# Layer 1's experts computed only for the two chosen per token, through a list sorted by expert

## The reference

```python
logits = jnp.einsum('th,eh->te', x, router_w)            # 8 experts
topk_logits, topk_idx = jax.lax.top_k(logits, K)         # K = 2
probs = jax.nn.softmax(topk_logits, axis=-1)
combine = combine.at[jnp.arange(T)[:, None], topk_idx].add(probs)
hmid = jax.nn.gelu(jnp.einsum('th,efh->etf', x, w1) + b1[:, None, :])   # 128 -> 256
y = jnp.einsum('etf,ehf->eth', hmid, w2) + b2[:, None, :]               # 256 -> 128
out = jnp.einsum('eth,te->th', y, combine)
```

## Time and profile before

| | |
|---|---|
| median of 3 runs | 1991.66 us (1989.51 to 1996.56) |
| profiled execution: span | 1994.7 us |
| token stage of layer 1, first matmul to the attention's first | 1142.1 to 1444.5 us |
| attention of layer 1 | 1444.5 us to the end |
| busy: PE, DVE, ACT, POOL | 86%, 67%, 60%, 57% of the span |
| HBM traffic | 67 GB/s over the span |

### The profile page before, as it was taken

One profiled execution on the slowest core, in us unless ns is written; L12 is line 12 of the kernel. 1 busy time (PEld: TensorE's weight loads), 2 busy tenths in 40 slices (PEclk: granted clock), 3 DMA queues, 4 the chain that ended last, 5 costly groups with the idle time before them and its releaser, 6 DMA issues. The chain is left out here.

```text
span 1994.7 us, 78600 instructions
## 1 busy us (share of the span) xinstructions
PE 1724.8 (86%) x34080; PEld 1310.1 (66%) x34080; DVE 1335.0 (67%) x1975; ACT 1194.0 (60%) x1438; POOL 1128.4 (57%) x1489
## 2 busy tenths in 40 slices
PE   6887789999999989999988689999967878788886
PEld 4666678777787777778766566667635555555554
DVE  5552777777777758877776244544477888777882
ACT  2333477777787768777876534444425656566565
POOL 4755589987899769987995522221012333334333
PEclk9988799999998999999998789999958999999898
DMA  3476032222322222222112122133112112121100
GB/s 111 124 212 173 24 96 76 76 71 76 88 69 80 62 76 83 86 70 70 48 59 69 58 68 82 58 91 97 54 26 50 31 49 48 37 59 31 26 24 17
DMA packets 166301, 139.91 MB, mean 70 GB/s; under 512 B 91715, under 2 KB 157014, under 8 KB 160454
## 3 DMA queue, kind: packets, MB, share of 16 engines
q1 hardware_dynamic: 150966, 100.40, 17.2%
q10 hardware_dynamic: 9616, 21.89, 4.5%
q0 software_dynamic: 5376, 12.59, 2.2%
HBM read 90.91 MB, written 43.12 MB: 67 GB/s over the span
## 5 line engine op out<-in xcount | busy, mean ns | idle before, releaser
L1364 ACT ACTIVATE a_EX<-bank 128x1024 f32<-128x1024 f32 x624 | 615.4, 1026 | 288.9 <-PE bank L1236 235.0
L1490 DVE TENSOR_TENSOR a_PM<-bank,a_PM 128x1024 f32<-128x1024 f32 x336 | 401.7, 1221 | 129.2 <-PE bank L1236 118.0
L1316 POOL TENSOR_TENSOR a_SN<-a_SN,a_MB 128x1024 f32<-128x1024 f32 x176 | 421.0, 2429 | 48.0 <-DMA a_MB<-m_dram 47.2
L1513 DVE TENSOR_REDUCE a_M<-bank 128x2 f32<-128x1024 f32 (+3 forms) x304 | 339.0, 1163 | 82.0 <-PE bank L1249 53.3
L1453 PE MATMUL bank<-a_EX,VV 128*32 128x128 f32 x9984 | 359.7, 288 | 6.5 <-issue 4.9
L1236 PE MATMUL bank<-QS,KS 51*128 51x128 bf16 (+1 forms) x4992 | 234.9, 228 | 93.9 <-DMA QS<-a_MP 29.9
L1453 PEld LDWEIGHTS bank<-a_EX,VV 128*32 128x32 f32 x9984 | 269.8, 114 | 51.0 <-issue 22.7
L1236 PEld LDWEIGHTS bank<-QS,KS 51*128 51x128 bf16 (+1 forms) x4992 | 156.7, 99 | 185.8 <-issue 52.0
L1360 ACT ACTIVATE a_SN<-bank 128x1024 f32<-128x1024 f32 x176 | 176.7, 1024 | 57.6 <-PE bank L1215 56.3
L1368 ACT ACTIVATE a_SN<-a_SN 128x1024 f32<-128x1024 f32 x176 | 184.9, 1060 | 34.7 <-POOL a_SN L1316 34.7
L1215 PE MATMUL bank<-QP,rel_t 112*128 112x32 bf16 x5632 | 197.9, 177 | 3.0 <-issue 2.7
(11 more groups left out here) (163 smaller groups left out, 2410.2 us busy)
## 6 DMA issues: line engine op xcount, KB each, us to landing
a_MB<-m_dram SPq DMA_DIRECT2D x32, 1024.0 KB, 5.0
QS<-q_dram SPq DMA_DIRECT2D x192, 96.0 KB, 2.9
KS<-k_dram ACTq DMA_DIRECT2D x16, 768.0 KB
q_dram<-t_PARTS SPq DMA_DIRECT2D x32, 192.0 KB, 2.8
k_dram<-t_PARTS SPq DMA_DIRECT2D x16, 384.0 KB, 2.9
QS<-a_MP SPq DMA_DIRECT2D x384, 2.0 KB
KR<-kr_dram ACTq DMA_DIRECT2D x8, 576.0 KB
q_dram<-t_PARTS SPq DMA_DIRECT2D x32, 128.0 KB, 2.6
```

What stands on the lines that cost most here:

```text
L1316: pool.tensor_tensor(near_view(sn), near_view(sn), as_near(MB[:, :, :], it.part), ALU.add)\
L1364: act.activation(as_banks(EX[:, it.need % ER[layer]], part), by_head, ACT.Exp, scale=SCALE).then_inc(act_done, 1)
L1490: dve.tensor_tensor(pm, mb.rearrange("p hh (k i) -> p hh k i", k=4), pm, ALU.max).then_inc(max_used, 1)
L1513: dve.tensor_reduce(target.rearrange("p (hh k) -> p hh k", hh=2)[:, :, p0:p0 + g], mb[:, :, 0:g * width].rearrange("p hh (k j) -> p hh k j ...
```

## The change

Layer 1's token stage is replaced (`routed_stage`); the other three stages keep their order. Layer 1's tokens are now normalised in two chunks of 2048 tokens (16 tiles) instead of groups of 512; the first chunk is prepared in the seam, the second one by DVE inside the stage. For each chunk, all logits come first; DVE picks the two experts for 16 tiles at once, and PE counts, with matmuls against tables of zeros and ones (`places`), where in a list sorted by expert each token's two copies go. Each expert's part of the list is filled up to whole tiles of 128 rows, so that the list has 39 tiles ("steps") per chunk, 78 in all, whatever the data. POOL scatters each tile of tokens twice into the list in DRAM, by 64 indirect transfers of 128 rows; the list was filled with zeros by 26 transfers of SP during layer 0's attention. Then the experts are computed step by step. SP loads the list four steps at a time (a "quad"), PE turns them, and the number of the expert of each step is read by PE, ACT and DVE from SBUF into registers, once per quad on each engine. DVE copies the expert's w1 (128x256) to a ring of four buffers for PE's weights; b1, w2 and b2 are addressed by register. DVE adds b2, SP stores the result. All of q, k and v, with their split, runs between the routing and the experts, with the differences of the split now on DVE. In the attention, POOL gathers a unit's two result rows per token with two indirect transfers and one plain one, four units ahead, mixes them (`mix`, three operations) and applies the silu with ACT's tanh (`gate`, two operations); DVE's multiplication in `final` waits for it. g_dram and the sum over 8 experts are gone for layer 1.

The diff, cut and moved to the left; first what is removed, then `routed_stage` in the order POOL, SP, ACT, PE, DVE, then the attention:

```diff
-if kind == "expert" and layer == 1:
-    if k + 1 < E:
-        hidden(f, p, k + 1)
-    elif not (f == GROUPS - 1):
...
-for t in range(GT):
-    y = bank[:, YB + k % 2, t * P:(t + 1) * P]
-    for h in range(2):
-        last = pe.matmul(y, HM[:, k % 2, h, t * P:(t + 1) * P], w2[:, k, h, :],
-                         start=h == 0, stop=h == 1)
...
-dve.wait_ge(y_psum, f * E + k + 1)
-for t in range(GT):
-    last = dve.scalar_tensor_tensor(ACC[:, p, t, :], bank[:, YB + k % 2, t * P:(t + 1) * P],
-                                    C[:, p, t, k:k + 1], ACC[:, p, t, :], ALU.mult, ALU.add)
...
+def experts_of(engine, c, q):
+    size = quad_size(q)
+    _, values = nc.values_load_multi_w_load_instructions(step_e[0:1, c, 4 * q:4 * q + size], engines=[engine],
+                                                         min_val=0, max_val=E - 1)
+    return values
...
+for c in range(CHUNKS):
+    pool.wait_ge(slots_ready, c + 1)
+    for t in range(CT):
+        for k in range(2):
+            at = SLOT[:, k, c * CT + t:c * CT + t + 1]
+            pool.indirect_dma_start(out=xs_dram[c], out_offset=bass.IndirectOffsetOnAxis(ap=at, axis=0),
+                                    in_=X1[c][:, t, :], in_offset=None).then_inc(scattered[c], 16)
...
+def load_slots(q):
+    c, i = divmod(q, QUADS)
+    sp.wait_ge(scattered[c], 16 * 2 * CT)
+    if q >= 3:
+        sp.wait_ge(xs_psum, q - 2)
+    size = quad_size(q)
+    sp.dma_start(XS[:, q % 3, 0:size, :], xs_dram[c].rearrange("(s p) d -> p s d", p=P)[:, 4 * i:4 * i + size, :])\
+      .then_inc(xs_in[q % 3], 16)
...
+for to, src in loads:
+    sp.dma_start(to, src).then_inc(route_in, 16)
+load_chunk(sp, 1)
+for to, src in expert_loads:
+    sp.dma_start(to, src).then_inc(expert_in, 16)
+sp.wait_ge(v_ones, 1)
+for f in range(GROUPS):
+    store_v(f)
+    store_qk(f)
+    if f == 5:
+        for q in range(3):
+            load_slots(q)
+for u in range(QR):
+    load_q(1, sp, u)
+for q in range(CHUNKS * QUADS):
+    store_y(q)
+    if q + 3 < CHUNKS * QUADS:
+        load_slots(q + 3)
...
+def first_part(f):
+    if f >= 2:
+        act.wait_ge(qk_stored[f % 2], QKS * (f // 2))
+    act.wait_ge(qk_taken, 2 * f + 2)
...
+for f in range(1, GROUPS):
+    values(f)
+    first_part(f)
+    second_part(f - 1)
+second_part(GROUPS - 1)
...
+if s >= 3:
+    act.wait_ge(y_psum, s - 2)
+for h in range(2):
+    last = act.activation(HM[:, s % 3, h, :], bank[:, HB + s % 3, h * P:(h + 1) * P], ACT.Gelu,
+                          bias=b1[:, bass.ds(e, 1), h:h + 1].rearrange("p a f -> p (a f)"))
+last.then_inc(hid_ready, 1)
...
+def hidden(q, k, s):
+    pe.wait_ge(xs_ready, q + 1)
+    pe.wait_ge(w_ready, s + 1)
+    if s >= 3:
+        pe.wait_ge(hid_ready, s - 2)
...
+for h in range(2):
+    last = pe.matmul(bank[:, HB + s % 3, h * P:(h + 1) * P], W[:, s % 4, h * P:(h + 1) * P], XST[:, q % 2, k, :],
+                     start=True, stop=True)
...
+def result(q, k, s, e):
+    pe.wait_ge(hid_ready, s + 1)
+    if s >= 3:
+        pe.wait_ge(y_ready, s - 2)
+    for h in range(2):
+        last = pe.matmul(bank[:, YB + s % 3, 0:P], HM[:, s % 3, h, :],
+                         w2[:, bass.ds(e, 1), h, :].rearrange("p a f -> p (a f)"), start=h == 0, stop=h == 1)
+    last.then_inc(y_psum, 1)
...
+for f in range(CG):
+    if f + 1 < CG:
+        turn(f + 1)
+    logits(f)
+project(0)
+pe.wait_ge(route_in, 16 * len(loads))
+places(0)
...
+for f in range(CG, GROUPS):
+    if f + 1 < GROUPS:
+        turn(f + 1)
+    logits(f)
+places(1)
+for f in range(1, GROUPS):
+    project(f)
...
+for i in range(QUADS):
+    q = c * QUADS + i
+    if q + 1 < CHUNKS * QUADS:
+        turn_slots(q + 1)
+    for k, e in enumerate(experts_of(mybir.EngineType.PE, c, i)):
+        s = step_index(c, 4 * i + k)
+        hidden(q, k, s)
+        if len(behind) == 2:
+            result(*behind.pop(0))
+        behind.append((q, k, s, e))
...
+def second_rest(f):
+    dve.wait_ge(p1_ready, f + 1)
+    dve.tensor_tensor(FR[:, f % 2, :, :], FQ[:, f % 2, :, :], PARTS[:, f % 2, 0, :, :], ALU.subtract).then_inc(r_ready, 1)
...
+def weights(s, e):
+    if s >= 4:
+        dve.wait_ge(hid_psum, s - 3)
+    dve.tensor_copy(W[:, s % 4, :], w1[:, bass.ds(e, 1), :].rearrange("p a f -> p (a f)")).then_inc(w_ready, 1)
...
+def add_bias(q, k, s, e):
...
+dve.tensor_tensor(Y[:, q % 3, k, :], bank[:, YB + s % 3, 0:P], b2[:, bass.ds(e, 1), :].rearrange("p a f -> p (a f)"),
+                  ALU.add).then_inc(y_ready, 1)
...
+dve.wait_ge(route_in, 16 * len(loads))
+route(0)
+chunk_statistics(dve, 1)
+dve.drain()
+rsqrt(dve, rstd1[:, :], var1[:, :], newton1[:, :], fused=True)
+chunk_normalise(dve, 1)
+dve.drain()
+route(1)
+for f in range(GROUPS):
+    take(f)
+    if f:
+        third_part(f - 1)
+    second_rest(f)
+third_part(GROUPS - 1)
...
+slots(q)
+for k, e in enumerate(experts_of(mybir.EngineType.DVE, c, i)):
+    s = step_index(c, 4 * i + k)
+    weights(s, e)
+    if len(behind) == 3:
+        add_bias(*behind.pop(0))
+    behind.append((q, k, s, e))
...
+if 2 <= u < 2 + CHUNKS * STEPS // 3:
+    sp.wait_ge(zeros_ready, 1)
+    c, s0 = divmod(3 * (u - 2), STEPS)
+    sp.dma_start(xs_dram[c].rearrange("(s p) d -> p s d", p=P)[:, s0:s0 + 3, :],
+                 bv[:, None, :].broadcast_to([P, 3, D])).then_inc(zeroed, 16)
...
+r, tile = u % XGR, row_of(u)
+for i in range(3):
+    pool.wait_ge(y_out[i], 16 * len(range(i, (tile // CT + 1) * QUADS, 3)))
+if u >= XGR:
+    pool.wait_ge(final_done, u - XGR + 1)
...
+for k in range(2):
+    pool.indirect_dma_start(out=XG[:, r, 1 + k, :], out_offset=None, in_=y_dram[tile // CT],
+                            in_offset=bass.IndirectOffsetOnAxis(ap=SLOT[:, k, tile:tile + 1], axis=0))\
+        .then_inc(xg_in[r], 16)
+pool.dma_start(XG[:, r, 0, :], x_v[tile]).then_inc(xg_in[r], 16)
...
+def mix(u):
+    r, tile = u % XGR, row_of(u)
+    pool.wait_ge(xg_in[r], 48 * (u // XGR + 1))
+    pool.tensor_scalar(XG[:, r, 1, :], XG[:, r, 1, :], PW[:, 0, tile:tile + 1], None, ALU.mult)
+    pool.tensor_scalar(XG[:, r, 2, :], XG[:, r, 2, :], PW[:, 1, tile:tile + 1], None, ALU.mult)
+    pool.drain()
+    pool.tensor_tensor(XG[:, r, 1, :], XG[:, r, 1, :], XG[:, r, 2, :], ALU.add).then_inc(z_ready, 1)
...
+def gate(u):
+    r = u % XGR
+    pool.wait_ge(th_ready, u + 1)
+    pool.tensor_tensor(XG[:, r, 2, :], TH[:, u % 2, :], XG[:, r, 1, :], ALU.mult)
+    pool.drain()
+    pool.tensor_tensor(XG[:, r, 1, :], XG[:, r, 1, :], XG[:, r, 2, :], ALU.add).then_inc(gate_ready, 1)
...
+if layer == 1 and u == 1:
+    mix(0)
+    mix(1)
...
+if layer == 1:
+    if u + 1 < UNITS:
+        gate(u + 1)
+    if u + XGR < UNITS:
+        load_xg(u + XGR)
+    if u + 2 < UNITS:
+        mix(u + 2)
...
+def tanh(u):
+    act.wait_ge(z_ready, u + 1)
+    if u >= 2:
+        act.wait_ge(gate_ready, u - 1)
+    act.activation(TH[:, u % 2, :], XG[:, u % XGR, 1, :], ACT.Tanh, scale=0.5).then_inc(th_ready, 1)
...
+dve.scalar_tensor_tensor(XO[:, r, :], bank[:, MISC, P:2 * P], 0.5, XG[:, u % XGR, 1, :],
+                         ALU.mult, ALU.mult).then_inc(misc_used, 1)
...
-statistics(dve, 1, X1, 0)
+chunk_statistics(dve, 0)
```

More of the change, by code:

```diff
@@ L876, in body @@
                     def body(kind, f, p, k):
-                        if kind == "expert" and layer == 0:
+                        if kind == "expert":
                             if k == 0 and f == 0:
@@ L1293, in _ @@
                     for r in range(2):
[L1294 removed]
+                        sp.wait_ge(stored[r], STORED1 * (layer + 1))
                 @block.gpsimd
@@ L1308, in _ @@
+                    for u in range(2 if layer == 0 else XGR):
+                        load_xg(u)
                     for it in plan["pool"]:
@@ L1392, in _ @@
                             act.activation(OT[:, :], bank[:, MISC, 0:P], ACT.Copy).then_inc(ot_ready, 1)
+                            if layer == 1 and 1 <= u < UNITS - 1:
+                                tanh(u + 1)
                 @block.tensor
@@ L1573, in build @@
             with ExitStack() as stage:
-                token_stage(layer, src, stage)
+                if layer == 0:
+                    token_stage(src, stage)
+                else:
+                    routed_stage(stage)
             with ExitStack() as stage:
```

763 lines of the change are left out of this document (500 added, 263 removed).

## The result

| | before | after |
|---|---|---|
| median | 1992.43 us (4 runs) | 2119.37 us (4 runs) |
| span of the profiled execution | 1994.7 us | 2121.5 us |
| first matmul of layer 1's token stage | 1142.1 | 1152.65 |
| length of that stage | 302.5 us | 340.5 us |
| attention of layer 1, to the end | 550.2 us | 628.4 us |

The changed kernel is slower: ratio 1.0621, 95% interval 1.0583 to 1.0658. I had said 1980 and a range up to 2035, so both the sign and the range were wrong. (The four runs of the kernel before are the three of the table ahead of the prediction and one more.) The difference of the two spans, 126.8 us, lies in three places: 10.6 ahead of the stage, 38.0 in it, 78.2 in the attention.

What follows compares the result with a forecast made beforehand. PE was taken to bound layer 1's token stage (302.5 us). Stage -33.5, seam +3, zero fills +1.5 and attention +17 gave -12 us, so 1980 for the median; forecast's own range 1960 to 2000, overall 1940 to 2035.

Steps and rivals of the forecast that it cites:

- Part 1: Routing in layer 1's token stage: first routing done at T+23, second at T+54, with almost nothing hiding it.
- T: First matmul of layer 1's token stage, the forecast's time zero; seam +3 and zero fills +1.5 us ahead of it.
- Part 2: q, k, v with their split: the two-buffer loop takes 11.5 us a group, ending at T+135.
- Part 3: The experts: PE leads with register reads on top, 1.65 us per step, 129 us for 78; stage ends T+269.
- The first rival: Experts: register reads cost nothing, covered by PE's queue; 1.2 us per step, 94 us, so 1945; chance 0.2.
- The third: Experts: half of them run at 1.2 GHz because PE pauses, 41 us more, so 2021; chance 0.12.
- Seam and zero fills: Ahead of the stage: larger normalisation +3 us; 26 zero fills in layer 0's attention +1.5 us, bounds 0 and 16.
- Attention: Layer 1's attention: POOL's longer loop +15 us and late first rows +2, together +17; gather priced at 1.2 us.
- one of the signs of being wrong: Attention: the forecast is wrong if PE waits for POOL's root (L1334) in most units.
- The second rival: Attention: POOL takes PE's place; at 2.43 us per gather the loss is 55 instead of 15, so 2020; chance 0.2.
- the loop: Attention: chain POOL, PE, ACT, PE, DVE from one POOL addition to the next, 14.4 us, a minimum for every interval.

Runs made afterwards that it cites:

- e8: e7 with POOL scattering only after both routings: 1988.8 us, ratio 0.999 to the kernel before.
- e9: e8 with the experts' numbers written into the program, so no register is read: 1953.4 us, ratio 0.978 to the kernel before.
- e7: e6 with three buffers instead of two for the split parts of q, k, v: 1998.8 us, ratio 1.001 to the kernel before.
- e1: The changed kernel with SP loading list tiles ahead of stores, and query loads after quad 3's store: 2039.1 us, ratio 1.023 to the kernel before.
- b2: The kernel before with two unused plain transfers of 128 rows per unit behind POOL's addition in layer 1's attention: 2033.3 us, ratio 1.020.
- e5: The changed kernel run again, unchanged: 2121.5 us, ratio 1.065 to the kernel before.
- e6: e1 with POOL's gate, mixing and transfers moved ahead of its wait for DVE's multiplication, transfers three units ahead: 2018.3 us, ratio 1.012 to the kernel before.
- b1: The kernel before with two unused gathers of 128 rows per unit behind POOL's addition in layer 1's attention: 2066.7 us, ratio 1.035.
- b3: The kernel before with b1's unused gathers issued ahead of POOL's wait for DVE's multiplication: 2029.6 us, ratio 1.019.
- f4: f3 with gate behind the addition, drains behind every second scatter pair, key/value loads spread over chunk 2's experts: 1974.2 us, ratio 0.989 to the kernel before.
- e4: The changed kernel with each unit's two gathers replaced by plain transfers of 128 rows: 2059.9 us, ratio 1.032 to the kernel before.
- f1: e7 with a POOL drain behind each pair of scatters: 1987.6 us, ratio 0.997 to the kernel before.
- f3: f1 with ACT's first key and value loads ahead of chunk 2's experts, not chunk 1's: 1995.1 us, ratio 1.001 to the kernel before.

## Why the prediction was wrong, step by step

**Part 1.** Right where semaphores came in time: T+21 for T+23 and T+51 for T+54. In the profile they came late, T+77: 23 us that no step had. The step that failed is a term put at nothing: the time between the end of a matmul and the start of what waits for it. "Turning and taking logits of four groups: 4 x (1.09 + 1.71) = 11 us" has none, and "PE turns at T+32 and has all logits at T+43" is where it stood. PE's semaphores rose late, for 26.5 us in all, while POOL issued scatters. I had asked only what these cost POOL. That it is the scatters rests on this: the delay is absent where only plain transfers run, and moves to the experts and to v when the scatters move (e8, e9). Why one chip doesn't show it is open.

**Part 2.** Right: 82 us for 81, 11.2 to 12.3 us a group for 11.5, and e7 shows that it was the double buffer.

**Part 3.** 181 us from the last third part to the stage's end, for 134. The step that failed is "So PE leads, with the register reads of each quad on top". The reads were 1.46 us for 2.0, and PE's work at the higher clock was 0.90 us a step and a quarter of 0.66 for the turns (1407.44 to 1408.34 above), as forecast. In e1 the part took 134.2 us, the number of the prediction, but that is partly luck: its steady step is 1.40 us for 1.65, which gives 78 x 1.40 + 5 = 114, and the other 20 are gaps that the prediction didn't have, 13 of them at the one quad that waited for its list tiles. In the changed kernel SP came ahead of PE: the load of a quad stood behind the store of another, and the last nine stores with their 17.8 us issue stood ahead of the first such load; e1's order took 47 us off. I had walked SP's program through the q, k, v part and left it out of the next, though the diff showed the order. The first rival (registers free) fell with e9. The third (lower clock) was true in part: 0.84 over the experts, where PE was busy for 104.4 us against 89.9 in e1, at 0.92. That is 14.5 us more work of PE inside the 47; it went with the waits when SP's order changed, and no run separates the two.

The Trainium skill's floor of 600 ns for a register's load (DMA: Bandwidth & Descriptors, "Latency and other measured facts") doesn't hold on PE, where the median of 20 is 0.33 us; on ACT and DVE it is 0.60 and 0.65. All four numbers came in one load, and DVE's register operations behind it took 1.1 us more before its first copy (1363.17 to 1364.28 in e1).

**Seam and zero fills.** T came 10.6 us later for 4.5. The seam gave 2.6 of these, for 3: from DVE's last reciprocal to the first matmul it took 8.3 us (1144.35 to 1152.65) and 5.7 before (1136.35 to 1142.09). The rest arose in layer 0's attention; over 14 profiles of kernels with the zero fills T lay between 1145 and 1158, over four without between 1138 and 1144. That the fills are the cause wasn't tested by itself.

**Attention.** +78 for +17. A gather cost 1.26 us with its gap, for 1.2, and POOL's block came out at 7.2 us, for 6.6: the prices were right. What failed is "but 15 are below 14.4, by 19 us together; letting later long ones catch up leaves 11". The 16 intervals above 14.4 us grew like the 15 others, by 2.7 us against 2.8, and the mean of all went from 15.9 to 18.6. The order is laid down for all engines: PE takes the turn of POOL's output at its place in the list or waits, and a wait of PE, busy 118 of 140 us, is not made up. So a delay of POOL's root is added, not compared with a slack in the mean. PE waited for it in 22 of the 32 units, one of the signs of being wrong that I had named. I also took a plain handoff after the transfers, where a drain stands, which lasts until they land: the two units where keys landed beside them grew by 10.5 and 9.8 us. The late releases, 25 us here, stood in no term of the sum, and neither did the lower clock in the attention, at which PE was busy 26 us longer.

**The second rival** named the right engine and the right wait, and ruled itself out by the price: "It decides from about 1.6 us per gather". By the loop, yes; by the order of the steps even b2's plain transfers, at 0.54 us each, cost 38 us. 0.2 was too little for it.

Summed over the spans: 6 us of the miss of 139 are in the seam and layer 0, 23 in the routing, 1 in q, k, v, 47 in the experts, 61 in the attention (50 us of PE's wait for the root and 25 of late releases, where the sum had 17 in all).

## What to carry to other kernels

When a change hands work to an engine whose order is laid down, ask where in its list the work stands and who waits for the next step, not how much room the engine has in the mean: the same 64 gathers cost 72 us behind a step and 33 ahead of one, and 37 of the 40 us between the two attentions are in one wait. Walk every queue's program through every part, the DMA-issuing engine's above all: a load behind a store of the same ring inherits the wait of that store. And don't follow a transfer with a drain on its own engine.

## What the runs showed of the hardware

- A drain on POOL behind its own transfers ended 0.1 to 0.4 us after the last of them had landed: 2 us after its issue in ordinary units, 10.9 us after it beside a load of 768 KB (b2).
- Where POOL issues indirect transfers, PE's semaphores can rise up to 18.5 us after the matmul that raises them has ended, and ACT and DVE start that much later. It occurs in every profile with indirect transfers of some groups (e5, e6, b1, b3, e7 to e9, f4, and the first one of the change); in others, e1 to e4, no release of the attention is over 0.3 us late, and in f1 to f3 the late ones come to 3 us at most. With plain transfers alone it doesn't occur (b2, the kernel before). The profiles that have indirect transfers and not the delay are all of one chip. Whether it is the chip, and what holds the release back, stays open.
- An indirect transfer of 128 rows of 512 bytes mostly occupies POOL for 0.96 us, with 0.3 between two, scatter and gather alike; a plain one for 0.54 to 0.61.
- Four numbers read into registers in one load, and used, cost 1.46 us a quad on the path (5.60 against 4.14). The load itself took 0.33 us on PE and 0.65 on DVE, whose reading PE waited for.
